# Local attention with shared window sums: one run of value products fewer per group, overlapping columns added by GpSimd, and a new time table

## The reference

```python
rel = k_idx - W - q_idx                       # W = 64
win = (rel >= -pad) & (rel <= pad - 1)        # pad = 32: a band of 64 keys
attn_local = softmax(where(valid & win, q.k * scale, NEG))
out_local = attn_local @ v
kg, vg = k[:, ::W], v[:, ::W]                 # 128 global keys per batch
out_global = softmax(q.kg * scale) @ vg
out = (out_local + out_global) @ w_out + b_out
```

## Time and profile before

| what | value |
|---|---|
| median of 3 runs | 3613.41 us (3602.11 to 3613.45) |
| the profiled execution: its own time | 3610.1 us |
| its span, first to last instruction | 3608.4 us |
| TensorE busy, whole span | 3540.8 us (98%) |
| VectorE, ScalarE, GpSimd busy | 2262.6, 1977.4 and 1935.8 us (63%, 55%, 54%) |
| mean granted TensorE clock | 0.988 |
| DMA | 571.22 MB, mean 158 GB/s |

### The profile page before, as it was taken

How to read it: one execution, slowest core, us unless ns; L and a number is a source line. 1 busy time by engine, 2 the same in 40 slices (tenths; PEclk the granted TensorE clock), 3 DMA queues, 4 the chain that set the end, 5 groups by cost and what they waited for, 6 DMA issues and landing times.

```text
span 3608.4 us, 77520 instructions
## 1 busy us (share of the span) xinstructions
PE 3540.8 (98%) x28482; PEld 2753.2 (76%) x28482; DVE 2262.6 (63%) x4672; ACT 1977.4 (55%) x4132; POOL 1935.8 (54%) x3091
## 2 busy tenths in 40 slices
PE   8999999999999899999999999999999999999997
PEld 6888888888888677777777777777777777777775
DVE  4333333333333477777777777777777777777774
ACT  3222222222222467677667767677777777677764
POOL 0000000000000367787787877887777878887787
PEclk9999999999999699999999999999999999999999
DMA  4545545455457666666666666666666666666651
GB/s 151 210 157 192 188 161 209 163 186 195 154 198 217 132 138 152 159 152 143 156 156 157 155 146 154 160 152 143 153 158 155 150 151 151 161 156 146 151 125 42
DMA packets 420885, 571.22 MB, mean 158 GB/s; under 512 B 41656, under 2 KB 187208, under 8 KB 420568
## 3 DMA queue, kind: packets, MB, share of 16 engines
q1 hardware_dynamic: 412024, 564.79, 59.9%
q10 hardware_dynamic: 8256, 2.16, 0.3%
q0 software_dynamic: 288, 0.08, 0.0%
HBM read 361.59 MB, written 203.23 MB: 157 GB/s over the span
## 4 chain that ended last, share of the span: by engine, by line
PE 62%; POOL 1%; ACTq 0%; ACT 0%; issue 0%; DVE 0%; DMA 0%; POOLq 0%; SPq 0%; DVEq 0%
PE ps_misc L1058 19%; PE ps_sc L998 7%; PE ps_ml L974 7%; PE ps_o L1030 6%; PE ps_mg L979 5%; PE ps_s L1030 4%; PE ps_sc L1012 4%; PE ps_o L1042 3%; PE ps_s L1036 3%; PE ps_sc L1067 2%; PE ps_sc L985 1%; PE ps_sc L1006 1%; ACTq L841 0%; POOL rsb L751 0%; DMA w_both<-mt 0%
## 5 line engine op out<-in xcount | busy, mean ns | idle before, releaser
L886 DVE TENSOR_REDUCE mx<-ps_ml 128x2 f32<-128x384 f32 x1024 | 561.7, 549 | 390.8 <-PE ps_ml L974 390.0
L451 PE MATMUL po<-ht_hi,w_both 128*128 128x512 f32 x2048 | 654.2, 393 | 1.5 <-ACT ht_hi L276 1.5
L846 ACT ACTIVATE ps_ml<-mask 128x384 f32<-128x384 bf16 x1022 | 501.9, 491 | 206.3 <-DVE mx L886 128.7
L818 ACT ACTIVATE qk<-ps_sc 128x384 f32<-128x384 f32 (+1 forms) x1024 | 416.8, 458 | 221.0 <-PE ps_sc L998 219.2
L451 PEld LDWEIGHTS po<-ht_hi,w_both 128*128 128x128 f32 x2048 | 385.2, 188 | 81.1 <-ACT ht_hi L276 1.8
L760 POOL TENSOR_SCALAR_AFFINE_SELECT qk<-qk 128x512 f32<-128x512 f32 (+1 forms) x512 | 298.2, 582 | 247.1 <-ACT qk L818 246.1
L889 DVE TENSOR_REDUCE mx<-ps_mg 128x2 f32<-128x256 f32 x1024 | 425.2, 415 | 1.9 <-PE ps_mg L979 1.9
L451 PE MATMUL po<-ht_lo,w_both 128*128 128x512 f32 x1024 | 399.3, 390 | 0.0
L831 ACT ACTIVATE v<-ps_sc 128x512 f32<-128x512 f32 x512 | 304.8, 596 | 94.1 <-PE ps_sc L1012 88.5
L763 POOL TENSOR_SCALAR_AFFINE_SELECT qk<-qk 128x512 f32<-128x512 f32 x512 | 326.0, 637 | 35.0
L455 PE MATMUL po<-w_both,ht_hi 128*128 128x512 f32 x1024 | 332.7, 396 | 0.0
(11 more groups left out here) (161 smaller groups left out, 8194.4 us busy)
## 6 DMA issues: line engine op xcount, KB each, us to landing
w_both<-q_hi_d SPq DMA_DIRECT2D x256, 256.0 KB
ks<-k_hi_d SPq DMA_DIRECT2D x128, 288.0 KB
xb<-in_L_attn_x SPq DMA_DIRECT2D x132, 256.0 KB, 2.9
q_lo_d<-o_lo SPq DMA_DIRECT2D x32, 1024.0 KB, 8.7
k_lo_d<-o_lo SPq DMA_DIRECT2D x32, 1024.0 KB, 10.1
w_both<-q_lo_d SPq DMA_DIRECT2D x128, 256.0 KB
vw<-v_d SPq DMA_DIRECT2D x128, 256.0 KB, 3.0
out<-xb SPq DMA_DIRECT2D x128, 256.0 KB, 3.3
```

What stands on the lines that cost most here:

```text
L451: last = nc.tensor.matmul(po[o % 6][:], wa[:, k, o * P:(o + 1) * P], ha[u][:, k, :], start=start, stop=stop)
L818: nc.scalar.activation(p_loc[:, i, 2 * hp:2 * hp + 2, lo:MW], ps_sc[n % 2][:, 0:2 * MW].rearrange("p (h n) -> p h n", h=2)[:, :, lo:MW], A ...
L846: nc.scalar.activation(ps_ml[u % 2][:, :, 0:MW], mask[:].rearrange("p (o n) -> p o n", o=1).to_broadcast([P, 2, MW]), ACT.Copy).then_inc(s ...
L886: nc.vector.tensor_reduce(mx[s % 2][:, 0, heads, tile], ps_ml[u % 2][:, :, 0:MW], axis=AX.X, op=ALU.max).then_inc(ml_taken, 1)
```

## The change

Three things. First, the sums: ps_s no longer gets every window as a whole. GpSimd adds, for each pair of neighbouring key tiles, the 64 columns in which their windows overlap into a new buffer p_sum (three adds a step, each right behind the selects of key tiles 1, 2 and 3), and TensorE multiplies only the columns that are left once. Second, the order: pvl 2, 3, 4 and pvgs stand next to each other in the table, so that tiles 2 and 3, the last keys and the global sums are one run; the four value products of a tile no longer alternate with sums. Third, a new table of times for everything.

```diff
+        p_sum = qk0[:].rearrange("p a n -> p (a n)")[:, 16 * MW:16 * MW + 12 * WIN].bitcast(F32).rearrange("p (i h n) -> p i h n", i=3, h=4)
-        VALUES = (("pvl", 0, 3.7999), ("pvl", 1, 3.8198), ("pvl", 2, 6.7674), ("pvl", 3, 7.039), ("pvl", 4, 7.8708),
-                  ("pvgs", 0, 8.1795), ("oc", 0, 8.3287), ("sums", 0, 9.1038), ("pvgo", 0, 9.6821), ("rglob", 0, 9.1995),
+        VALUES = (("pvl", 0, 3.7407), ("pvl", 1, 3.7417), ("pvl", 2, 7.6064), ("pvl", 3, 7.6074), ("pvl", 4, 7.6084),
+                  ("pvgs", 0, 7.6094), ("oc", 0, 9.0215), ("sums", 0, 8.5752), ("pvgo", 0, 9.6825), ("rglob", 0, 9.491),
...
                         pool.affine_select(late, late, [[0, 4], [-1, P]], ALU.is_ge, 0.0, base=0, channel_multiplier=1).then_inc(loc_masked, 1)
+                        if i > 0:
+                            pool.wait_ge(loc_masked, 5 * s + i + 1)
+                            pool.tensor_tensor(p_sum[:, i - 1, :, :], p_loc[:, i - 1, :, P:MW], p_loc[:, i, :, 0:WIN], ALU.add).then_inc(s_added, 1)
...
-                        at_least(act, pvl_done, 5 * (s - 1) + i + 1)
+                        at_least(act, pvl_done, 5 * (s - 1) + (2 if i < 2 else 4))
+                        if i == 1:
+                            at_least(act, s_added, 3 * (s - 1) + 2)
...
                         pe.wait_ge(loc_masked, 5 * s + i + 1)
-                        for dst, vals in ((ps_o, vw[g]), (ps_s, None)):
+                        if i in (1, 3):
+                            pe.wait_ge(s_added, 3 * s + i)
+                        for h in range(4):
...
+                        halves = ps_s[:].rearrange("p (t b n) -> p t b n", b=2, n=WIN)
+                        parts = {1: ((halves[:, 0:2, 0, :], p_loc[:, 0:2, :, WIN:P]), (halves[:, 0, 1, :], p_sum[:, 0, :, :])),
+                                 3: ((halves[:, 2, 0, :], p_loc[:, 2, :, WIN:P]), (halves[:, 1:3, 1, :], p_sum[:, 1:3, :, :]),
+                                     (ps_s[:, CHUNK - P:CHUNK], p_loc[:, 3, :, WIN:MW])),
+                                 4: ((ps_s[:, CHUNK - WIN:CHUNK], p_last[:]),)}.get(i, ())
+                        for n, (sums, windows) in enumerate(parts):
                             for h in range(4):
+                                window = windows[:, :, h, :] if len(windows.shape) == 4 else windows[:, h, :]
+                                last = nc.tensor.matmul(sums[h * DH:(h + 1) * DH], ones[0:windows.shape[0], 0, :], window,
+                                                        start=i == 1 and n == 0, stop=False, skip_group_check=True)
                         last.then_inc(pvl_done, 1)
```

More of the change, by code:

```diff
@@ L630, in attention_phase @@
         sc_scored, sc_exped = sem("sc_scored"), sem("sc_exped")
[L631 removed]
+        early_cut, loc_masked, s_added = sem("early_cut"), sem("loc_masked"), sem("s_added")
         pvl_done, pvgs_done, pvgo_done = sem("pvl_done"), sem("pvgs_done"), sem("pvgo_done")
@@ new lines, in attention_phase @@
+        TAKEN = 0.1055
+        SEED = (1.0271, 0.4068, 0.2215, 1.1484, 0.8669, 1.04, 0.8495, 1.242)
+        SCORES = (("mt", 0, -4.2567), ("loc", 0, -0.8982), ("loc", 1, 0.5075), ("loc", 2, 1.5738), ("loc", 3, 4.5985),
+                  ("last", 0, 5.8429), ("glob", 0, 1.9051), ("glob", 1, 2.8396), ("glob", 2, 2.8416), ("glob", 3, 4.9395))
+        VALUES = (("pvl", 0, 3.7407), ("pvl", 1, 3.7417), ("pvl", 2, 7.6064), ("pvl", 3, 7.6074), ("pvl", 4, 7.6084),
+                  ("pvgs", 0, 7.6094), ("oc", 0, 9.0215), ("sums", 0, 8.5752), ("pvgo", 0, 9.6825), ("rglob", 0, 9.491),
+                  ("og", 0, 9.8762), ("rloc", 0, 11.512), ("ol", 0, 12.4963), ("osum", 0, 13.1253))
@@ L1019, in item @@
                         pe.wait_ge(loc_masked, 5 * s + i + 1)
-                        for dst, vals in ((ps_o, vw[g]), (ps_s, None)):
-                            for h in range(4):
-                                if i < 4:
-                                    x0, w = (0, P) if i == 0 else (P * i - WIN, MW)
-                                    lhs = ones[:, 0, :] if vals is None else vals[:, i, h * DH:(h + 1) * DH]
-                                    rhs = p_loc[:, i, h, MW - w:MW]
-                                else:
-                                    x0, w = CHUNK - WIN, WIN
-                                    lhs = ones[0:WIN, 0, :] if vals is None else vl[g][:, h * DH:(h + 1) * DH]
-                                    rhs = p_last[:, h, :]
-                                last = nc.tensor.matmul(dst[h * DH:(h + 1) * DH, x0:x0 + w], lhs, rhs,
-                                                        start=i == 0, stop=i == 4 and dst is ps_o, skip_group_check=True)
+                        if i in (1, 3):
+                            pe.wait_ge(s_added, 3 * s + i)
@@ new lines, in item @@
+                        for h in range(4):
+                            rows, head = slice(h * DH, (h + 1) * DH), slice(h * DH, (h + 1) * DH)
+                            if i < 4:
+                                x0, w = (0, P) if i == 0 else (P * i - WIN, MW)
+                                last = nc.tensor.matmul(ps_o[rows, x0:x0 + w], vw[g][:, i, head], p_loc[:, i, h, MW - w:MW],
+                                                        start=i == 0, stop=False, skip_group_check=True)
+                            else:
+                                last = nc.tensor.matmul(ps_o[rows, CHUNK - WIN:CHUNK], vl[g][:, head], p_last[:, h, :],
+                                                        start=False, stop=True, skip_group_check=True)
```

21 lines of the change are left out of this document (8 added, 13 removed).

## The result

| kernel | median of 3 | runs | ratio to before, 95% interval |
|---|---|---|---|
| before | 3613.41 us | 3602.11 to 3613.45 | |
| after | 3654.47 us | 3653.22 to 3655.80 | 1.0119 [1.0100, 1.0138] |

The change makes the kernel 41 us slower; 41 us faster was forecast. The profiled execution of after has a span of 3651.2 us. Of the 41 us, 96 x 0.37 = 36 lie in these steps.

A forecast was written before the change was run, and what follows sets the result against it. TensorE bounded the kernel before at 18.33 us a step; after, GpSimd at about 18.02 would. Saving 120 x 0.31 + 8 x 0.52 = 41 us from 3610.1 gave 3569, stated as 3570 us, with 3538 to 3594 for 8 in 10.

The forecast's parts named there:

- TensorE's sum is then 18.33 - 0.29 - 0.23 = 17.81 us a step: TensorE's step in the second phase: shorter sums save 0.29 us and joining runs 0.23, 0.52 in all.
- GpSimd's load: Three adds a step on GpSimd, 0.73 us each, raise its own work from 15.6 to 18.0 us a step.
- TensorE's terms: TensorE's two savings a step: 0.29 us from shorter sums and 0.23 us from one run of 32-column products fewer.
- 0.67 in the joined run: Sums over 64, 2x64 and 128 columns in TensorE's joined run, with the row change: 0.67 us predicted.
- shorter sums: TensorE's local sums without the doubled overlap columns: 1.21 us a step becomes 0.92, 0.29 saved.
- one run fewer: One run of 32-column products fewer on TensorE saves 0.33 us a step, net 0.23 after a row-change charge.
- the 0.10 at the row change: Charge inside TensorE's joined run where products change from 128 to 64 rows: 0.10 us, zero as other bound.
- I add 0.02 us a step: Allowance for GpSimd's remaining waits for other engines once it is full: 0.02 us a step.
- Rival 2: GpSimd's waits do not vanish; with 0.2 us a step left the kernel takes 3590 us; chance 0.17.
- Rival 1: GpSimd has just room enough, so TensorE's full 0.52 us a step comes: 3543 us; chance 0.27.
- Rival 3: TensorE's waits, in lumps of 1.2 us, bring the clock down to half: 3661 us, slower; chance 0.08.
- Putting the adds on GpSimd: Placing the three adds on GpSimd; with them on VectorE, the step was said to stay at TensorE's 17.81 us.

The follow-up runs named there:

- experiment 1: After without GpSimd's three adds a step and the waits for them, overlap sums leaving out one part: 3646.34 us.
- 13: After without adds, with pvl 2 and 3 back at their old places so that the run is split in two: 3671.30 us.
- experiment 9: The changed kernel's code with the old table and its separate runs, without the adds and their waits: 3566.86 us.
- experiment 7: The changed kernel's code with the joined run placed in the old table, without the adds and their waits: 3630.62 us.
- 8: After with one table number moved, the global score of key tile 3 from 4.9395 to 5.6 units: 3645.28 us.
- 16: After without adds, with the global score of key tile 3 moved from 4.9395 to 5.6 units: 3634.73 us.
- 14: Changed code without adds, old table with joined run, and maximum product 4 moved from 7.31 to 7.86 units: 3652.50 us.
- 2: After without adds and with the old sums over each key tile's whole window, new table and joined run kept: 3690.82 us.
- experiment 5: The changed kernel's code, adds on GpSimd and shorter sums, with every time of the old table and separate runs: 3657.11 us.
- experiment 11: After with the addition of epsilon, three times a step, moved from GpSimd to VectorE: 3658.76 us.
- Experiment 3: After with the three adds a step moved from GpSimd to VectorE, at places of their own in the table: 3819.80 us.

## Why the prediction was wrong

**The step that failed** is "TensorE's sum is then 18.33 - 0.29 - 0.23 = 17.81 us a step". It counts the durations of what is removed and joined, and lets every other distance stand as in the old order. The table that came with the change moves nearly every item, and I costed that at nothing beyond GpSimd's load. In the new order products stand 0.73 us a step above their least distances even without adds (experiment 1; 0.09 before), more than the 0.52 that it was to save. The same code differs by 104 us between the two tables (13 against 9), and joining the run inside the old table costs 64 us (7 against 9) where a gain of 29 was expected. A value run was work that kept TensorE busy while VectorE reduced and ScalarE emptied banks; taken out of its place, it uncovers these.

**Its place, in part.** The largest single wait, 0.39 us a step, is the global score of tile 3, three feed-forward products behind the local scores of its key tile. The distance before and after could be read from the two orders and set beside ScalarE's 1.15 us of DMA issue. Putting it back gave 9 and 12 us (8 and 16), little more than the noise and far less than 0.39 x 128 = 50. The other 0.4 us lie in several places and move when one is mended (8, 14, 16). Which set of positions would be gapless with the joined run was not found, and whether there is one stays open.

**TensorE's terms** held where they stand alone: sums 0.66 us for 0.67 in the joined run, shorter sums 44 us (2 against 1) and 43 (9 against before) for 37, one run fewer 25 for 29, the last with a wait mixed in and both with some 10 us of noise. Their sum of 17.81 us a step was reached by no kernel; the nearest is 18.02 (experiment 9). The Trainium skill, "TensorEngine Tiling (Array Packing)", section "Key Properties", on the drain at a change of mode, stands with the 25 us and the 0.10 at the row change; no run measures that drain by itself.

**GpSimd's load** held: add 734 ns for 0.73, own work 18.02 and 18.06 us a step for 18.0. What failed is a **second step**, "I add 0.02 us a step" for its waits. With both engines at the same load (GpSimd 18.06 us a step in experiment 5, TensorE 18.02 in 9) each one still waits for the other in turn: 0.5 us a step. So in the old order the new code loses too (3657). Rival 2 was the nearest case; it had this mechanism, with 0.2 to 0.3 us of leftover, and only 0.17 of the chance. In after its mechanism is not what decides, for relieving GpSimd gives nothing there (experiment 11).

**Rival 1** needed room on GpSimd; experiment 9 gives it that room by leaving the adds out and comes to 3567, not 3543; its run is not joined. With the run joined as well it is 3631 (experiment 7), so room on GpSimd was not enough. **Rival 3** is refuted for the steady part of after (clock 1.00). Its premise, a wait of 1.20 us and then a clock of 0.50, does not hold in every run either: experiment 9 waits 1.21 us at the same place and the clock stays at 1.00 for the next 15 us.

The Trainium skill, "GPSIMD Engine Reference", section "Engine selection", spoke for VectorE. Experiment 3 agrees for an add that meets no long GpSimd instruction: 415 ns there against 734 on GpSimd. For the others it does not, and the Trainium skill has the reason, "SBUF — State Buffer", section "SBUF: two separate sides": a VectorE instruction with two SBUF inputs and a GpSimd one that reads SBUF exclude each other from a shared port, for the whole instruction. The trace agrees, with 1310 ns on average for the 112 adds that were held, while VectorE's add of 512 elements with one input in PSUM takes 690 to 694 ns in the same kernel, though GpSimd is busy during it. Putting the adds on GpSimd is not the step that failed, since without any adds the new order loses too (experiment 1).

## What to carry to other kernels

In a gapless in-order schedule an item is worth its duration only where it stands. Before costing a new order by its sums, take the two or three products that now stand closer to the producer of their input or to the reader of their bank, and set the new distance beside what that engine has to do in between, its DMA issues included. And two engines that are both nearly full don't run at the larger of their sums: here half a microsecond a step of mutual waiting was left, as much as the change had to give. A mean can hide two kinds: before an engine is called slow for an instruction, look at its single times and at what the other engines did then.

## What was unexpected of the hardware

- VectorE's add of 128x256 with both inputs in SBUF took 415 ns beside an idle GpSimd, or one at a 128x1 instruction, and 1310 ns on average (up to 1.93 us) when it began inside a longer GpSimd instruction. Its add of 128x512 with one input in PSUM took 692 ns even then.
- Issuing two small DMAs held ScalarE's own stream for 1.15 us; its exponential, and through it a PSUM bank, came late for that.
- The same wait of TensorE in the first steps of the phase came before either clock. In the kernel before (1.20 us) and in experiment 5 (1.20 and 0.74 us) the stretch from 1235 to 1250 us followed at a granted clock of 0.50 (1.2 GHz). In experiment 9 the 15 us behind a wait of 1.21 us were at 1.00 (2.4 GHz); the wait, then the stretch, columns as above:

```profile
1229.24 0.47 PE L975 MATMUL ps_ml<-ks,w_both 97*128 97x192 f32 x2 [1.21 <-ACT ps_ml L847]
```

```profile
1230.00:1245.00 15.00, 13.29 (x163) 9.41 (x162) 9.88 (x22) 9.86 (x24) 7.69 (x11) 1.00 0.76 153
```

What decides between the two was not found. In the steady part of after, with some 0.8 us of excess spread over each step, the clock stayed at 1.00.
